# Second attention block: the memory update as one product over keys and negated keys, reads moved between two maxima, signed parts and normalization moved

## The reference, cut to what matters

```python
def step(carry, qkv):                       # one of 4 segments of 64 rows
    M, z = carry                            # memory, 16 heads
    q, k, v = qkv
    sq = _sigma(q)                          # elu + 1
    denom_q = jnp.sum(sq * z[:, :, None, :], axis=-1, keepdims=True) + EPS
    A_mem = jnp.matmul(sq, M) / denom_q     # what the queries read
    scores = jnp.matmul(q, jnp.swapaxes(k, -2, -1)) * inv_sqrt_dk
    scores = jnp.where(causal, -jnp.inf, scores)
    A_dot = jnp.matmul(jax.nn.softmax(scores, axis=-1), v)
    A_s = beta * A_mem + (1.0 - beta) * A_dot
    sk = _sigma(k)
    denom_k = jnp.sum(sk * z[:, :, None, :], axis=-1, keepdims=True) + EPS
    V_prev = jnp.matmul(sk, M) / denom_k    # what the keys read
    M_new = M + jnp.einsum('bhtk,bhtv->bhkv', sk, v - V_prev)
    z_new = z + jnp.sum(sk, axis=-2)
    return ((M_new, z_new), A_s)
```

## Time and profile before

| | |
|---|---|
| median of 3 runs | 1736.06 us |
| the profiled execution | 1733.57 us |
| its span | 1731.8 us |
| busy over the span | PE 87%, PEld 74%, DVE 78%, ACT 47%, POOL 51% |
| block B | from about 1000 us to the end, 732 us |
| mean granted TensorE clock in block B | 0.92 of full |
| DMA in block B | busy 31%, 92 GB/s |

### The profile page before, as it was taken

How to read it: one execution, slowest core, us unless ns; L and a number is a source line. 1 busy time by engine, 2 the same in 40 slices (tenths; PEclk the granted TensorE clock), 3 DMA queues, 4 the chain that set the end, 5 groups by cost and what they waited for, 6 DMA issues and landing times. The chain is left out here.

```text
span 1731.8 us, 46136 instructions
## 1 busy us (share of the span) xinstructions
PE 1501.8 (87%) x13668; PEld 1285.4 (74%) x13668; DVE 1354.8 (78%) x3426; ACT 813.1 (47%) x1859; POOL 880.2 (51%) x1180
## 2 busy tenths in 40 slices
PE   5999999999999999996687648888888888888887
PEld 4999898998898998995566436666666666666665
DVE  5589999999999999995345366788887877788874
ACT  1556666665665666664466523333333333333331
POOL 4365565665566665654688543333343433333331
PEclk9999999999999999998799868999999999999997
DMA  4432233322222322220444232333333333333330
GB/s 141 142 94 89 78 82 91 91 81 74 81 82 91 91 76 76 80 76 15 136 124 132 58 93 86 96 99 100 98 102 97 101 97 100 98 101 100 94 92 17
DMA packets 181694, 158.10 MB, mean 91 GB/s; under 512 B 12529, under 2 KB 163185, under 8 KB 181618
## 3 DMA queue, kind: packets, MB, share of 16 engines
q1 hardware_dynamic: 181618, 157.17, 31.3%
HBM read 113.09 MB, written 44.04 MB: 91 GB/s over the span
## 5 line engine op out<-in xcount | busy, mean ns | idle before, releaser
L587 PE MATMUL a_bank<-a_vp,a_prob 128*128 128x96 f32 x4096 | 635.2, 261 | 0.0
L587 PEld LDWEIGHTS a_bank<-a_vp,a_prob 128*128 128x128 f32 x4096 | 610.7, 192 | 5.6
L481 ACT ACTIVATE a_prob<-a_bank 128x512 f32<-128x512 f32 x512 | 305.9, 598 | 267.9 <-PE a_bank L571 267.0
L675 DVE TENSOR_REDUCE a_nmax<-a_bank 128x2 f32<-128x512 f32 x512 | 345.1, 680 | 47.7 <-PE a_bank L556 40.7
L556 PE MATMUL a_bank<-a_k_st,a_q_st 96*128 96x256 bf16 x1024 | 259.2, 276 | 36.3 <-DVE a_nmax L675 35.1
L571 PE MATMUL a_bank<-a_q_st,a_k_st 120*128 120x256 bf16 x1024 | 281.7, 276 | 3.2 <-POOL a_q_st L344 3.2
L1613 PE MATMUL c_o_bank<-c_vb,c_prob 128*128 128x96 f32 x1024 | 176.6, 297 | 30.1 <-DVE c_ad L1896 29.3
L344 POOL TENSOR_SCALAR a_q_st<-a_mt 24x2048 bf16<-24x2048 bf16 x64 | 121.4, 1896 | 138.9 <-PE a_bank L571 94.8
L1771 DVE TENSOR_REDUCE c_nmax<-c_bank 128x4 f32<-128x512 f32 x256 | 165.0, 681 | 31.4 <-PE c_bank L1583 29.9
L1487 ACT ACTIVATE c_prob<-c_bank 128x256 f32<-128x256 f32 x256 | 98.8, 386 | 176.2 <-PE c_bank L1563 174.5
L1613 PEld LDWEIGHTS c_o_bank<-c_vb,c_prob 128*128 128x128 f32 x1024 | 141.1, 199 | 41.4 <-DVE c_ad L1896 29.1
(11 more groups left out here) (202 smaller groups left out, 2999.8 us busy)
## 6 DMA issues: line engine op xcount, KB each, us to landing
a_q_st<-scratch_a_parts_dram SPq DMA_DIRECT2D x64, 288.0 KB
a_k_st<-scratch_a_parts_dram SPq DMA_DIRECT2D x192, 96.0 KB
c_q_st<-scratch_c_parts_dram SPq DMA_DIRECT2D x64, 288.0 KB
c_k_st<-scratch_c_parts_dram SPq DMA_DIRECT2D x192, 96.0 KB
scratch_a_parts_dram<-a_parts SPq DMA_DIRECT2D x32, 384.0 KB, 2.7
scratch_c_parts_dram<-c_parts SPq DMA_DIRECT2D x32, 384.0 KB, 2.7
a_x<-in_x SPq DMA_DIRECT2D x32, 128.0 KB, 3.2
scratch_y<-a_y SPq DMA_DIRECT2D x32, 128.0 KB, 2.7
```

The source lines that it names most:

```text
L481: act.activation(prob[h % 4][:, :, :].rearrange("p a b -> p (a b)"), t_ps[h % 2][:, :], ACT.Exp).then_inc(exped, 1)
L587: mm = pe.matmul(o_ps[g % 2][:, at:at + VC], prob[h % 4][:, c, t * P:(t + 1) * P], vp[o][:, c, :], start=c == 0, stop=c == NT - 1)
L675: dve.tensor_reduce(nmax[:, t, 2 * g:2 * g + 2], s_ps[t][:, :].rearrange("p (h k) -> p h k", h=2), AX.X, ALU.max, negate=True).then_inc(ma ...
```

## The change

1. The update product now has 128 rows that count: `skn` holds the keys in rows 0 to 63 and the negated keys in rows 64 to 127 (a second copy by ScalarE, with a factor of -1); `uv` holds the values above and the keys' read below. So VectorE writes the keys' read straight from PSUM into `uv`, the queries' read into `am` (two instructions of 64 rows), and the subtraction of L1808 is gone. TensorE waits for both before it overwrites `ps_c`.
2. VectorE does the first two reads between the two maxima of slots 2 and 4; the third stays in slot 6.
3. `pos` moves from slot 1 to slot 2 between the first maximum and the read, `neg` behind the second maximum.
4. z is written by ScalarE in slot 6 as x times rs plus shift, with shift = -mean x rs made by GpSimd in two small instructions more in `norm(0, ...)`.

```diff
+        negm, shift = sb("negm", [P, NT]), sb("shift", [P, NT])
...
                 pool.tensor_scalar(var[k][:, :], mv[k][:, :, 1], EPS, 1.0, ALU.add, ALU.mult).then_inc(norm_d[k], 1)
+                if k == 0:
+                    pool.tensor_scalar(negm[:, :], mv[0][:, :, 0], -1.0, 1.0, ALU.mult, ALU.mult
+                                       ).then_inc(norm_d[0], 1)
+                    pool.wait_ge(norm_d[0], NORM * b + 2)
+                    pool.tensor_tensor(rs[0][:, :], var[0][:, :], half[:, :], ALU.pow).then_inc(norm_d[0], 1)
+                    pool.wait_ge(norm_d[0], NORM * b + 3)
+                    pool.tensor_tensor(shift[:, :], negm[:, :], rs[0][:, :], ALU.mult).then_inc(norm_d[0], 1)
+                    return
...
                         act.copy(skn[0:SEG, :, :].rearrange("p s f -> p (s f)"),
                                  ps_c[0:SEG, 0:(NS - 1) * P]).then_inc(sk_d, 1)
+                        act.mul(skn[SEG:P, 1:NS - 1, :].rearrange("p s f -> p (s f)"),
+                                ps_c[0:SEG, P:(NS - 1) * P], -1.0).then_inc(sk_d, 1)
...
+                    if s == 6 and active(j, u, -1):
+                        act.wait_ge(norm_d[0], NORM * (n + 2))
+                        if later(j, n, 1):
+                            act.wait_ge(zt_p, n)
+                        for t in range(NT):
+                            act.activation(z[1 - i][:, t, :], x[1 - i][:, t, :], ACT.Identity,
+                                           scale=rs[0][:, t:t + 1], bias=shift[:, t:t + 1]).then_inc(z_d, 1)
...
                         if c == 0:
-                            pe.wait_ge(sk_d, b + 1)
+                            pe.wait_ge(sk_d, 2 * (b + 1))
                             pe.wait_ge(vs_d, b + 1)
                         else:
                             pe.wait_ge(u_d, b * 2 + c)
+                            pe.wait_ge(read_d, b * 9 + 3 * c)
...
                     elif k == 2:
-                        dve.tensor_tensor(by_head(am[o][:, c, :]), by_head(ps_c[:, 0:HV]),
-                                          dr[:, c, :].unsqueeze(2).broadcast_to([P, H, HD]), ALU.mult
+                        if c < 2:
+                            dve.tensor_tensor(by_head(uv[o][SEG:P, c + 1, 0:HV]),
+                                              by_head(ps_c[0:SEG, 0:HV]),
+                                              dr[0:SEG, c, :].unsqueeze(2).broadcast_to([SEG, H, HD]), ALU.mult
+                                              ).then_inc(u_d, 1)
+                        dve.tensor_tensor(by_head(am[o][SEG:P, c, :]), by_head(ps_c[SEG:P, 0:HV]),
+                                          dr[SEG:P, c, :].unsqueeze(2).broadcast_to([SEG, H, HD]), ALU.mult
                                           ).then_inc(read_d, 1)
-                    elif c < 2:
-                        dve.tensor_tensor(uv[o][0:SEG, c + 1, 0:HV], uv[o][0:SEG, c + 1, 0:HV],
-                                          am[o][0:SEG, c, :], ALU.subtract).then_inc(u_d, 1)
...
                     if s in S_AT and active(j, u, 1):
-                        for t in range(NT):
-                            reduce_unit(S_AT.index(s), t)
+                        reduce_unit(S_AT.index(s), 0)
+                    if s == 2 and active(j, u, 0):
+                        dve.wait_ge(kq_d, (n + 1) * 2)
+                        if later(j, n, 1):
+                            dve.wait_ge(sg_d, n)
+                        signed(pos, ALU.max)
+                    if s in S_AT and active(j, u, 1):
+                        if s in (2, 4):
+                            for k in range(3):
+                                read(s // 2 - 1, k)
+                        reduce_unit(S_AT.index(s), 1)
+                    if s == 2:
+                        signed(neg, ALU.min)
...
-                    if s == 7 and active(j, u, -1):
-                        if later(j, n, 1):
-                            dve.wait_ge(zt_p, n)
-                        normed(0, n + 1, x[o], z[o], z_d)
```

More of the change, by code:

```diff
@@ L1274, in attention_b @@
         flat = lambda a: a[:, :, :].rearrange("p c f -> p (c f)")
-        N_LOAD, N_LATE, SPLIT, MP, AD, VD = 3, 4, 4, 8, 6, 4
+        N_LOAD, N_LATE, SPLIT, MP, AD, VD, NORM = 3, 4, 4, 8, 6, 4, 4
         MT_AT = (3, 7)
@@ L1455, in body @@
                 if isinstance(j, int) and -1 <= n < 1:
-                    pool.wait_ge(norm_d[0], 2 * (n + 2))
+                    pool.wait_ge(norm_d[0], NORM * (n + 2))
                     value_consts(n + 1)
@@ L1803, in read, with signed @@
                     elif k == 2:
-                        dve.tensor_tensor(by_head(am[o][:, c, :]), by_head(ps_c[:, 0:HV]),
-                                          dr[:, c, :].unsqueeze(2).broadcast_to([P, H, HD]), ALU.mult
+                        if c < 2:
[5 more added lines that the diff above has]
+                                          dr[SEG:P, c, :].unsqueeze(2).broadcast_to([SEG, H, HD]), ALU.mult
                                           ).then_inc(read_d, 1)
-                    elif c < 2:
-                        dve.tensor_tensor(uv[o][0:SEG, c + 1, 0:HV], uv[o][0:SEG, c + 1, 0:HV],
-                                          am[o][0:SEG, c, :], ALU.subtract).then_inc(u_d, 1)
+                def signed(dst, op):
+                    if active(j, u, 0):
+                        dve.tensor_scalar(flat(dst), ps_a[:, :], 0.0, None, op).then_inc(pn_d, 1)
                 if isinstance(j, int) and n == 0:
@@ L1827, in body @@
                         if later(j, n, 0):
-                            dve.wait_ge(norm_d[0], 2 * (n + 1))
+                            dve.wait_ge(norm_d[0], NORM * (n + 1))
                         moments(0, n + 1, x[o])
@@ L1838, in body @@
                             remember(s // 2, k)
-                    if s == 4 and active(j, u, 1):
-                        for k in range(4):
-                            read(1, k)
                     if s == 6 and active(j, u, 1):
@@ L1845, in body @@
                             split_max(1, k)
[L1846 to L1849, removed]
+                            if k < 3:
+                                read(2, k)
                     if s == 2 and active(j, u, 3):
@@ L1861, in body @@
                         moments(1, b, x3[o])
-                    if s == 1 and active(j, u, 0):
-                        dve.wait_ge(kq_d, (n + 1) * 2)
-                        if later(j, n, 1):
-                            dve.wait_ge(sg_d, n)
-                        dve.tensor_scalar(flat(pos), ps_a[:, :], 0.0, None, ALU.max).then_inc(pn_d, 1)
-                        dve.tensor_scalar(flat(neg), ps_a[:, :], 0.0, None, ALU.min).then_inc(pn_d, 1)
                     if s == 6 and active(j, u, 3):
```

## The result

The changed kernel takes **1760.2 us** (median of four runs, 1757.61 to 1761.25) against 1736.2 us for the kernel before on the same chip: ratio **1.0151**, interval 1.0132 to 1.0169. It is slower, as forecast, and inside the range, but by 24 us where the forecast said 12: twice the effect. The profiled execution took 1761.25 us (span 1759.5), 27.7 more than that of before. PE is busy 86%, DVE 76%, ACT 48%, POOL 51%; the mean granted clock of 1063 to 1664 us is 0.95, as before.

What follows compares the result with a forecast made beforehand. TensorE was busiest, VectorE's serving order decisive. Step: 20.28 + 0.28 + 1.12 - 0.43 = 21.25 against 21.52; with 0.8 clock loss, over 31 steps +16.4, minus 2 at the start: 1733.6 to 1748 us, range 1712 to 1768.

Steps and rivals of the forecast that it cites:

- Subtraction gone: Keys' read comes from PSUM, so the 0.99 us of the slow step should go; new step priced from 20.28.
- Slot 4, the new wait: Second unit of slot 5 waits 1.12 us for slot 4's second maximum, now behind the read, priced at 1.08.
- z: z on ScalarE lets VectorE start the reciprocals earlier: gain 0.43 us, all in the wait before the next step.
- Slot 2 and 3: VectorE's run up to the split maxima starts 0.20 later, is otherwise the same plus 0.08: step loses 0.28 us.
- The two products of 64 rows: Two products replace one of 128 rows and a subtraction: 0.30 us each, read 1.08 us instead of 1.01.
- The place of that wait: TensorE's slot 3 idle was forecast as one piece of 1.53 us before the transpose of the split maxima.
- The clock: Clock falls behind three of four steps, about 1.1 us each: 0.8 us a step, range 0 to 1.49.
- The rival that the second maximum is not on the path: Slot 4's 1.12 us wait falls away: 1689 to 1713 us, deciding at 1.1 us from product end to maximum; chance 0.15.
- That the clock holds: Rival: everything as forecast but no clock fall, 1723 us; chance 0.22.
- The z4 rival: GpSimd's earlier sum for `sg` stretches VectorE's scaling of z4, 0.6 us a step more: 1767 us; chance 0.10.

Runs made afterwards that it cites:

- product alone: Kernel before with only the update product over keys and negated keys, z still on VectorE and VectorE's old order: 1708.1 us, ratio 0.9836.
- z-alone run: Kernel before with only z moved to ScalarE, subtraction and VectorE's old order kept: 1739.2 us, ratio 1.0031.
- full-rows run on the changed order: Changed kernel with the queries' read taken over all 128 rows, nothing else: 1735.0 us, ratio 0.9996.
- z and product in the old order: Kernel before plus new product and z on ScalarE, VectorE's order unchanged: 1695.2 us; with the queries' read over all 128 rows (the 19.83 us step): 1683.4 us.
- slot 4 back: Changed kernel with the read of slot 4 put back behind the second maximum: 1709.9 us, ratio 0.9865.
- slot 4 swapped: Kernel before plus product and z, VectorE's old order except the read ahead of the second maximum in slot 4 only: 1728.6 us, ratio 0.9964.
- slot 2 back: Changed kernel with the read of slot 2 put back behind the second maximum, slot 4 still swapped: 1747.9 us, ratio 1.0089.

## Why the prediction was right or wrong

The direction was right and the size was not: 1761.25 us for the profiled execution against 1748. Step by step, for the step without a fall:

- **Subtraction gone: right.** No product is stretched, and the product alone gives 1708.1. As the z-alone run shows, it is also what made the move of z pay.
- **Slot 4, the new wait: right, 1.02 for 1.12**, and the swap alone adds 1.0 us to a step. The read took 1.14 us (1344.52 to 1345.66) instead of the 1.08 priced. From the transposes of slot 3 on the step grows by 1.20, not counting what z gains; the other 0.2 is not the swap's, since the product alone loses as much between these transposes and slot 6.
- **z: right, -0.48 for -0.43.**
- **Slot 2 and 3: this step failed.** "All that follows up to the last of the split is the same work plus 0.08" holds for the work but not for its time. It takes 0.22 more (0.12 in the read, 0.11 at `x3`), and with the 0.20 of the later start the step loses 0.42, not 0.28. The cause is the start row: I applied it to the pair and to the maximum behind it, not to `x3` two instructions later. The full-rows run on the changed order takes most of both back (0.09 and 0.11).
- **The two products of 64 rows: the same cause, and the largest miss.** The sum has 0.08 us for them in slot 2 and, inside the 1.12, 0.07 in slot 4; to the read of slot 6, whose product also starts in row 64 now, it gives nothing. Measured alone they cost 0.35 a step (20.63 against 20.28), and over full rows nothing: z and product in the old order take 19.83 then, which is 20.28 less the 0.48 of z and 0.03.
- **The place of that wait.** I put it in one piece before the transposes. Three quarters of it stand before the value products, whose bank `x3` empties; I had not asked for each TensorE instruction between which of VectorE's it waits for.
- **The clock: its cost near, its base not.** The mean step has 0.91 us of it, against 0.8. But I expected falls of 1.1 us behind three of four steps; there are 13 in 28, and they cost 1.45 to 3.8. Two errors cancelled, and that the sum came near is luck. The 1.1 stood on a slow stretch that lies beside the new wait of slot 5. It does not: all eleven falls of 3.4 us have ended before TensorE begins that wait, as here (it waits from 1323.93; the first line as in the earlier trace rows):

```profile
1319.70:1323.10 3.40, 3.40 (x23) 2.52 (x21) 1.07 (x4) 1.05 (x3) 2.69 (x5) 0.53 0.25 88
```

```profile
1324.95 0.39 PE L1598 MATMUL c_bank<-c_causal,c_ident 128*128 128x512 bf16 x1 [1.02 <-DVE c_nmax L1790]
```

Nor does the wait in slot 3 decide by its length, as I had read the earlier trace rows: with slot 4 back the same idle there goes with 4 falls, not 13.

One change after the other, from the kernel before to the changed one, the steps without a fall grow by 0.35 (product), -0.48 (z), 1.0 (slot 4 swapped), 0.32 (signed parts later: slot 2 back against slot 4 swapped) and 0 (slot 2 swapped), 1.19 in all; the changed kernel shows 1.18. The forecast had 0.15, -0.43, 1.05, 0.20 and 0, together 0.97.

The 13.3 us between forecast and profile: slot 2 to 5 and z, 1.18 - 0.97 = 0.21 us a step, 6.5 over 31 steps; the clock, 0.11 a step, 3.4; the mean of before, 21.48 and not 21.52, 1.2; and the first and last steps, +0.1 beyond the 31 where -2 was forecast, 2.1.

The rival that the second maximum is not on the path is refuted by its 1.02 us in every step. From `dn` (1344.52) to the end of the maximum (1346.35) the rows show 1.83 us. The 1.1 at which I let it decide was itself misread: by the rows the wait goes only when this is down to 0.7, since TensorE is ready 0.74 behind the product (1312.68 to 1313.42). The run that takes it off (slot 4 back, 1709.9) lies at the edge of the range that this rival gave, 1689 to 1713. That the clock holds is refuted by 13 falls. The z4 rival did not happen in the changed kernel, but its mechanism is real.

What stays open: which pattern of idle pieces brings the clock down. The table gives the counts; no experiment moved the two pieces apart in time while their lengths stayed, and each count is from one profiled execution.

## What to carry to other kernels

Before an instruction is moved ahead on an engine that relays between two stages, ask of each instruction that it displaces which bank that one frees and when that bank is next written: the same swap was free in slot 2 and cost 1.0 us a step in slot 4. Time several parts of such a change apart: here product and z gave 40 us, and the order took 65 back. And when a step gets shorter, look at what now meets on VectorE and GpSimd; one semaphore on the engine with time to spare can keep them apart (1689.8 to 1670.7).

## What was not expected of the hardware

- The start row of an instruction on VectorE mattered more than its rows: 128 rows from row 0 are 12 us faster over the kernel than 64 rows from row 64 on, and the delay can also fall on a later one, here `x3`, with a maximum and `neg` in between.
- GpSimd stretched a scaling of 128x128 with two pointers from SBUF to SBUF as well: two took 1.68 us instead of 0.60. The rule that the prediction cites beside this rival, from "SBUF — State Buffer" of the Trainium skill, section "Who interferes with whom", gives the ports that the two share to whichever comes first, for its whole instruction. By that rule, the trace agrees, the second z4 ends just behind `sg`, at 1311.81 against 1311.72; and in an early step of the same run (z4 from 1088.54, `sg` from 1088.65) z4 keeps its 0.34 us and `sg` takes 1.36 instead of 1.27.
- With 1.7 us idle in slot 3 and 1.0 in slot 5, some 4 us behind it, the clock fell in 13 of 28 steps; with the first alone in 4, with 1.25 and 1.0 in 1.
